# Selective scan: one third of the u*B inputs made by ScalarE and TensorE, 18 of 32 products with C on GpSimd

## The reference, cut to what matters

```python
def step(h, inp):
    dt_t, B_t, C_t, x_t = inp
    dA = jnp.exp(dt_t[..., None] * A)
    h = dA * h + (dt_t * x_t)[..., None] * B_t[:, None, :]
    y = jnp.einsum('bds,bs->bd', h, C_t)
    return (h, y)
```

## Time and profile before

| | us |
|---|---|
| median of 3 runs | 933.68 (931.17 to 933.75) |
| the profiled execution | 933.33 |
| its span | 931.5 |
| mean granted PE clock | 0.92 of full |

### The profile page before, as it was taken

One profiled execution on the slowest core, in us unless ns is written; L12 is line 12 of the kernel. 1 busy time (PEld: TensorE's weight loads), 2 busy tenths in 40 slices (PEclk: granted clock), 3 DMA queues, 4 the chain that ended last, 5 costly groups with the idle time before them and its releaser, 6 DMA issues. The chain is left out here.

```text
span 931.5 us, 13443 instructions
## 1 busy us (share of the span) xinstructions
PE 769.6 (83%) x3784; PEld 504.4 (54%) x3784; DVE 764.1 (82%) x1265; ACT 543.2 (58%) x1309; POOL 652.2 (70%) x447
## 2 busy tenths in 40 slices
PE   4889887899999994787878788786988767777998
PEld 2566653566666662435554465454645554422786
DVE  3588867668889995848989899998999989999743
ACT  1588854544444441676778776676875776552332
POOL 3178850467777782239989989999998999995000
PEclk9899998799999997997978699889998978899999
DMA  3000007499879836316557545655456555552001
GB/s 116 1 1 1 0 16 316 162 421 357 298 272 362 310 132 200 73 48 166 154 153 198 169 130 158 185 143 162 143 161 174 158 154 156 169 156 67 1 1 46
DMA packets 66307, 141.76 MB, mean 152 GB/s; under 512 B 11649, under 2 KB 22273, under 8 KB 64065
## 3 DMA queue, kind: packets, MB, share of 16 engines
q1 hardware_dynamic: 56432, 117.62, 41.6%
q0 software_dynamic: 6048, 18.59, 5.6%
q10 hardware_dynamic: 3760, 4.78, 1.5%
HBM read 129.92 MB, written 11.04 MB: 151 GB/s over the span
## 5 line engine op out<-in xcount | busy, mean ns | idle before, releaser
L2078 POOL TENSOR_TENSOR uB<-u,rows_B 128x1024 f32<-128x1024 f32 x127 | 298.4, 2359 | 0.0
L2296 DVE TENSOR_TENSOR_SCAN da<-da,uB 128x512 f32<-128x512 f32 x160 | 193.2, 1220 | 20.6 <-ACT da L2180 19.3
L2321 PE MATMUL ya<-ident,hV 128*128 128x128 f32 x560 | 100.0, 311 | 45.7 <-DVE hV L2195 45.5
L2088 POOL TENSOR_TENSOR hP<-hS,rows_C 128x512 f32<-128x512 f32 x96 | 122.2, 1273 | 18.2 <-DVE hS L2293 12.2
L2321 PEld LDWEIGHTS ya<-ident,hV 128*128 128x128 f32 x560 | 74.7, 159 | 97.7 <-DVE hV L2195 68.8
L2293 DVE TENSOR_TENSOR_SCAN hS<-da,uB 128x512 f32<-128x512 f32 x96 | 115.8, 1206 | 7.1 <-issue 3.7
L2195 DVE TENSOR_TENSOR hV<-da,rows_C 128x512 f32<-128x512 f32 x160 | 107.0, 669 | 0.6 <-DMA rows_C<-bc_rows 0.6
L1139 POOL DMA_INDIRECT xg<-x_rows,li x63 | 73.2, 1161 | 46.6 <-DVE li L1001 22.6
L1230 PE MATMUL gups<-wring,xT 128*128 128x448 f32 x252 | 105.0, 539 | 0.3 <-issue 0.3
L2179 ACT ACTIVATE da<-zero 128x2 f32<-128x2 f32 x160 | 27.7, 173 | 126.4 <-DVE hV L2195 125.7
L2180 ACT ACTIVATE da<-dt,fm_A 128x510 f32<-128x510 f32 x128 | 85.1, 674 | 0.0
(11 more groups left out here) (419 smaller groups left out, 1692.5 us busy)
## 6 DMA issues: line engine op xcount, KB each, us to landing
rows_B<-bc_rows SPq DMA_DIRECT2D x128, 256.0 KB, 3.7
rows_C<-bc_rows SPq DMA_DIRECT2D x128, 256.0 KB, 4.3
wring<-in_moe_own SPq DMA_DIRECT2D x31, 704.0 KB, 6.2
wring<-in_moe_two SPq DMA_DIRECT2D x16, 1024.0 KB, 15.1
rows_sum<-y_rows SPq DMA_DIRECT2D x6, 512.0 KB, 8.4
lut_i<-in_lut_idx SPq DMA_DIRECT2D x1, 2160.0 KB, 8.6
x_rows<-xnw ACTq DMA_DIRECT2D x1, 1280.0 KB, 5.2
x<-in_x SPq DMA_DIRECT2D x4, 256.0 KB, 3.7
```

What stands on the lines that cost most here:

```text
L2078: e.tensor_tensor(uB[:, r % UPAIRS, :, :], u[:, d:d + 2, :], RB[:, r % BROWS, :].unsqueeze(1).broadcast_to([P, 2, HALF]), ALU.mult).then_i ...
L2088: e.tensor_tensor(hP[:, k % PBUF, :], hS[:, k % HBUF, :], RC[:, row % CROWS, :], ALU.mult).then_inc(s_hp, 1)
L2296: e.tensor_tensor_scan(a[:, way], a[:, way], uB[:, r % UPAIRS, b, way], 0.0, ALU.mult, ALU.add).then_inc(s_sc, 1)
L2321: mm = e.matmul(ya[n % 2][:, part], at[:, part], g.ident[:, :], start=False, stop=False, is_transpose=True, skip_group_check=True)
```

## The change

Only the scan changes.

1. In segments 1 to 3, for states 4, 7, 10, 13 and 14 of each pair (`TURNED`), POOL no longer makes u*B and SP no longer loads the row of B. PE turns u of both blocks (columns become partitions), ACT keeps that as `uT` and the turned B as `bT`. Then ACT makes the turned u*B, four copies of 128x256 with a scale per partition, into `uBT` (2 buffers). PE turns it back, four transposes per step, into the bank `da` that is three steps old (`input_back`).
2. For these steps the decay goes to SBUF (`das`, 3 buffers), and the scan takes decay from SBUF and input from PSUM.
3. In segments 1 to 3 POOL takes 18 of the 32 products with C of a pair instead of 12. PE adds them BACK = 5 steps later instead of 4. CBUF falls from 4 to 3, HBUF rises from 4 to 5, PBUF and LATE stay.
4. The space comes from `lutw`: the table is stored to HBM by SP ahead of the first row and loaded again by ACT's queue at step 2 of the last segment, where the weights' inputs `hh` and `hl` lay.
5. silu(z) of a segment moves from step 1 of its own to step 29 of it, directly ahead of silu(x) of the next, which moves from 33 to 29.

```diff
-UPAIRS, CBUF, PBUF, DABUF, HBUF = 3, 4, 3, 3, 4
-LATE = 4
+UPAIRS, CBUF, PBUF, DABUF, HBUF = 3, 3, 3, 3, 5
+FIRST_TURNED, TURNED, UTBUF, DSBUF = 1, (4, 7, 10, 13, 14), 2, 3
+LATE, BACK = 4, 5
 def on_pool(n):
-    return n % PSTEP % 7 in (1, 3, 5) and n % PSTEP < PSTEP - LATE
+    m = n % PSTEP
+    if m >= PSTEP - LATE:
+        return False
+    return m % 7 in (1, 3, 5) if n // SSTEP < FIRST_TURNED else m % 3 != 2 and m > 0
+def turned_row(r):
+    return 2 * r // SSTEP >= FIRST_TURNED and r % DS in TURNED
 def summed(pair):
+    first, end = pair * PSTEP, (pair + 1) * PSTEP
     order = []
-    for n in range(pair * PSTEP, (pair + 1) * PSTEP):
-        if not on_pool(n):
-            order.append(n)
-        if n - LATE >= pair * PSTEP and on_pool(n - LATE):
-            order.append(n - LATE)
+    for n in range(first, end + BACK):
+        if n < end and not on_pool(n):
+            order.append((n, n))
+        if n - BACK >= first and on_pool(n - BACK):
+            order.append((n, n - BACK))
     return order
...
+        def turns_tensor(e, seg):
+            if seg >= FIRST_TURNED:
+                yield 0
+                turn_u(e, 2 * seg, 0)
+                yield 29
+                turn_u(e, 2 * seg + 1, 0)
+                yield 31
+                turn_u(e, 2 * seg + 1, 1)
+            if FIRST_TURNED <= seg + 1 < NSEG:
+                yield 62
+                turn_rows(e, seg + 1)
+                yield 63
+                turn_u(e, 2 * seg + 2, 1)
+        def turns_scalar(e, seg):
+            if seg >= FIRST_TURNED:
+                yield 0
+                keep_u(e, 2 * seg, 1)
+                yield 2
+                keep_u(e, 2 * seg, 0)
+                yield from turned_scalar(e, 2 * seg)
+                yield 31
+                keep_u(e, 2 * seg + 1, 0)
+                yield 33
+                keep_u(e, 2 * seg + 1, 1)
+                yield from turned_scalar(e, 2 * seg + 1)
+            if FIRST_TURNED <= seg + 1 < NSEG:
+                yield 63
+                keep_rows(e, seg + 1)
...
+        def turned_input(e, row, q):
+            t, seg = TROWS.index(row), 2 * row // SSTEP
+            if q == 0:
+                e.wait_ge(s_ut, 2 * TURN_PAIRS.index(row // DS) + 2)
+                e.wait_ge(s_bt, seg - FIRST_TURNED + 1)
+                if t >= UTBUF:
+                    e.wait_ge(s_tr, 2 * (t - UTBUF) + 2)
+            s = row % DS
+            i = e.activation(sc.uBT[:, t % UTBUF, q, :], sc.uT[:, q, :, :].rearrange("p b d -> p (b d)"), ACT.Identity,
+                             scale=sc.bT[:, q, s:s + 1])
+            if q == HALF // P - 1:
+                i.then_inc(s_ub2, 1)
+        def turned_scalar(e, pair):
+            base = pair % 2 * PSTEP
+            for s in TURNED:
+                for q in range(HALF // P):
+                    yield base + 2 * s - 5 + q
+                    turned_input(e, pair * DS + s, q)
+        def input_back(e, n):
+            t = TSTEPS.index(n)
+            e.wait_ge(s_ub2, t // 2 + 1)
+            bank_free(e, n - DABUF)
+            for q in range(HALF // P):
+                mm = e.transpose(da[n % DABUF][:, q * P:(q + 1) * P], sc.uBT[:, t // 2 % UTBUF, q, n % 2 * P:(n % 2 + 1) * P],
+                                 g.ident[:, :])
+            mm.then_inc(s_tr, 1)
...
@@ project_scalar
+            if k > FIRST_TURNED:
+                yield 29
+                silu_z(e, k - 1)
+                silu_input(e, k)
             yield 31
             keep_dt(e, k - 1, 3)
-            yield 33
-            silu_input(e, k)
+            if k <= FIRST_TURNED:
+                yield 33
+                silu_input(e, k)
...
@@ the adds on PE
-                    begun = 0
-                    for i, n in enumerate(summed(pair)):
+                    begun, next_turned = 0, [n for n in TSTEPS if n // PSTEP == pair]
+                    for i, (at, n) in enumerate(summed(pair)):
+                        while next_turned and next_turned[0] - DABUF <= at:
+                            input_back(e, next_turned.pop(0))
```

More of the change, by code:

```diff
@@ L1306, in on_pool, with turned_rows, plain_rows @@
 def on_pool(n):
-    return n % PSTEP % 7 in (1, 3, 5) and n % PSTEP < PSTEP - LATE
+    m = n % PSTEP
+    if m >= PSTEP - LATE:
+        return False
+    return m % 7 in (1, 3, 5) if n // SSTEP < FIRST_TURNED else m % 3 != 2 and m > 0
 def pool_steps(n):
-    full, part = divmod(n, PSTEP)
-    return full * sum(on_pool(i) for i in range(PSTEP)) + sum(on_pool(i) for i in range(part))
+    return sum(on_pool(i) for i in range(n))
 def vector_steps(n):
     return n - pool_steps(n)
+def turned_row(r):
+    return 2 * r // SSTEP >= FIRST_TURNED and r % DS in TURNED
+def turned_rows(r):
+    return sum(turned_row(i) for i in range(r))
+def plain_rows(r):
+    return r - turned_rows(r)
 def place(n):
@@ L1404, in mamba @@
         XB = [S0, S1]
+        UTB = [[S1, S0], [S1, S1]]
+        TURN_PAIRS = range(2 * FIRST_TURNED, 2 * NSEG)
         INB = [[S0, S1], [S2, da[0]]]
@@ L1408, in mamba @@
         HB = NB // NH
-        mv, sm = c.sb(ctx, "ln3_mv", [P, NB, 2]), c.sb(ctx, "ln3_sm", [P, 4, NB])
+        mv, sm = c.over("ln3_mv", [P, NB, 2], sc.rest), c.over("ln3_sm", [P, 4, NB], sc.rest, skip=8 * NB)
         half_of = lambda seg: slice(seg % 2 * HALF, (seg % 2 + 1) * HALF)
@@ L1726, in diagonals, with bank_free, turn_u @@
                              scale=ws[1].cvw[:, m, t:t + 1]).then_inc(s_dg, 1)
+        def bank_free(e, past):
+            if on_pool(past):
+                e.wait_ge(s_sc, past + 1)
+            else:
+                e.wait_ge(s_hv, vector_steps(past + 1))
+        def turn_u(e, pair, b):
+            seg, d = pair // 2, 2 * (pair % 2) + b
+            at, to = TURN_PAIRS.index(pair), UTB[pair % 2][b]
+            e.wait_ge(s_u, DB * seg + d + 1)
+            if pair % 2 == 0:
+                e.wait_ge(s_dtc, DB * seg + d + 1)
+                if b == 0:
+                    e.wait_ge(s_bt, seg - FIRST_TURNED + 1)
+            elif b == 0 and seg + 1 < NSEG:
+                e.wait_ge(s_cv, DB * (seg + 1))
+            elif b:
+                e.wait_ge(s_ut, 2 * at + 1)
+            for q in range(HALF // P):
+                part = slice(q * P, (q + 1) * P)
+                mm = e.matmul(to[:, part], u[:, d, part], g.ident[:, :], start=q == 0, stop=True, is_transpose=True,
+                              skip_group_check=True)
+            mm.then_inc(s_tu, 1)
@@ L2757, in build, with in_table @@
             sc.yT = c.sb(mm, "y_turned", [P, 2, HALF])
+            spare_at = c.at[g.lutw.name]
+            def in_table(name, shape):
+                nonlocal spare_at
+                made = nc.alloc_sbuf_tensor_at(name, shape, F32, offset=spare_at)
+                spare_at += 4 * int(np.prod(shape[1:]))
+                assert spare_at <= c.at[g.lutw.name] + c.size[g.lutw.name]
+                return made
+            sc.uT = in_table("u_turned", [P, HALF // P, 2, P])
+            sc.uBT = in_table("uB_turned", [P, UTBUF, HALF // P, 2 * P])
+            sc.das = [in_table(f"decay{i}", [P, HALF]) for i in range(DSBUF - 1)]
             at = 0
```

117 lines of the change are left out of this document (89 added, 28 removed).

## The result

The changed kernel takes **1065.94 us** (1062.46 to 1068.03, 4 runs) against 933.71 for the kernel before (4 runs): the ratio is 1.1434, 95% interval 1.1403 to 1.1465. The forecast was slower, 980 us with a range of 938 to 1008. The direction was right and so was the wait that it named; the size was off by 86 us, and where that came from is worked out behind the experiments.

The account below looks back on a forecast made before the run. POOL and DVE were taken to bound the kernel. A pair walked to 58.9 us, plus 2 for side tasks and 1 for turned u, made 61.9; six pairs added 46.8 to 933.3, giving 980.1 us, range 938 to 1008.

Parts of the forecast that it names:

- What bounds the kernel now: Scan stretch, 417 to 852 us: POOL (416.0 of 435 us) and DVE (406.5) are both within 7% of full.
- the walk: One pair of channel blocks in segments 1 to 3, summed step by step: 58.9 us against 54.1 before.
- What is taken away and added: Six changed pairs: POOL falls by 25.3 us, DVE by 21.2; ACT's scaled copies add 56, PE's 60 transpose sets 26 to 40.
- The wait that the change turns on: With three buffers, POOL's products with C wait for PE's adds behind later DVE products: at least 12.1 us per six steps.
- The failed term is PE's part of the loop: Between DVE's product and POOL's: transposes back, two adds and signals, within 3.59 us from scan 12 to POOL's start.
- the loop: Scan 12 to 18 and 18 to 24: DVE product, PE's adds, POOL's products, next scan; at least 12.1 us each.
- The rest of the pair: Scan 24 to next 12: 11.3 us to 30, 3.6 to next pair, 6.7 to 4, 13.1 to 12.
- A: The loop isn't there in the six pairs; POOL's sum rules, 25.2 us less, 908 us; chance 0.13.
- B: The loop holds only scan 12 to 24, other 20 steps at POOL's price: 933 to 960 us; chance 0.16.
- C: In-order queues of PE and ACT bind beyond the loop: 65 to 66 us a pair, 1000 to 1010 us; chance 0.11.
- The sign that it named: In the scan stretch, PE over 95% busy or DVE waiting mainly for ACT or PE would show C.
- Signs: Right if POOL idles tens of us for PE, gates stand about 60 us apart, POOL's share falls to some 80%.

Follow-up runs that it names:

- four buffers: Changed kernel with four instead of three buffers for POOL's products with C and one hS buffer fewer (PBUF 4, HBUF 4): 968.05 us, ratio 1.038.
- PE awake, order mended: Changed kernel plus zero matmuls ahead of transposes back, both steps turned back at once, side tasks behind both adds; three buffers, BACK 5: 1051.18 us, ratio 1.112.
- best kernel: Changed kernel with PBUF 4, HBUF 5, DSBUF 2, BACK 4, both steps back at once, side tasks behind both adds, turned u kept later: 955.03 us, ratio 1.0103.
- kernel with PE awake: Changed kernel with three matmuls of zeros on PE ahead of each turned row's transposes back: 1060.23 us, ratio 1.1256.

## Why the prediction was off, step by step

By stretches of a pair, mean of six, worked out from the start of every scan (the last pair up to the end of its last scan):

| us | scan 0 to 4 | 4 to 12 | 12 to 18 | 18 to 24 | 24 to 30 | 30 to next 0 | pair |
|---|---|---|---|---|---|---|---|
| before | 9.9 | 11.6 | 9.6 | 9.6 | 10.0 | 3.4 | 54.1 |
| walked in the prediction | 6.7 | 13.1 | 12.1 | 12.1 | 11.3 | 3.6 | 58.9 |
| after | 8.8 | 14.9 | 15.0 | 15.1 | 15.8 | 5.4 | 75.0 |
| four buffers | 8.1 | 11.7 | 10.4 | 10.4 | 13.1 | 5.6 | 59.2 |
| BACK 4 | 8.2 | 13.2 | 10.4 | 10.6 | 12.4 | 4.5 | 59.3 |
| PE awake, order mended | 8.4 | 14.9 | 13.0 | 13.3 | 15.7 | 5.7 | 71.0 |
| best kernel (BACK 4, four buffers) | 8.3 | 11.0 | 10.1 | 9.8 | 12.3 | 3.7 | 55.1 |

**What bounds the kernel now.** Right: POOL and DVE at the top, POOL's waits for PE small.

**Where the miss lies.** A pair was forecast at 61.9 us (58.9 walked, 3 on top) and took 75.0. Against the walk 16.1 us are missing: 5.9 in the two loops from scan 12 to 24, 4.5 from 24 to 30, and 5.7 at the change of pair and in steps 4 to 12.

**What is taken away and added.** Right for POOL, the scans and ACT. The work on POOL fell by 23.7 us in the stretch (25.3 forecast), and the scans kept their length with their operands exchanged. ACT's copies took 58.4 us (56). PE was priced too low: its 60 sets back were busy 45.5 us where 26 to 40 were forecast, and all of its work in the stretch 397.7 where the most was 387. The silus were booked at 0 and are worth 6 us.

**The wait that the change turns on.** Right, and shown from two sides. A fourth buffer takes 94.9 us out of S and BACK 4 takes 93.9, each with the lower clock's share in it, and without turned rows the loop stays (S = 422.4).

**The failed term is PE's part of the loop.** It was walked as 1.79 us between the end of the DVE product and POOL's start, plus 0.4 for side tasks on average, and it measured 4.82 (646.82 to 651.64). Over all twelve loops the part from the scan to POOL is 2.3 us longer than walked. The prices came from rows in which PE had the upper clock, as its transposes 0.43 us apart in the earlier trace rows do, and the walk priced the last pair's adds, 1.02 us as plain matmuls in the kernel before, as transposes too; and though the page shows granted clocks of 0.7 to 0.9 by slice, the sum did not ask which clock PE would have just there. The loop itself makes PE idle ahead of it. Of the 3.0 us that a loop is longer than walked, the clock holds 1.3 to 1.9 (kernel with PE awake) and the side tasks 0.8 to 1.1; with the second transposes moved as well the loop falls to 12.5 in segments 1 and 2. The Trainium skill (TensorE: Matmul & The Clock Gate, Part 1) says that an idle TensorE drops to half its clock and gets it back by sustained work; the trace agrees (0.50 right behind 3.81 us of idle time), and the page was not weighed in the prediction.

**The rest of the pair.** Scan 24 to the next 12 was walked to 34.7 us and measured 44.9. With four buffers it is 38.4, so about 6 us of the gap go with the loop, and in the best kernel 35.3. One link that the walk left out can be read in pair 3. It took the DVE product of step 26 to end 5.8 us after scan 24, and it ended 10.84 after: DVE may issue it only behind scan 27, and scan 27 waited for its transposes back, which stood on PE behind the add of 23, side tasks and the add of 18:

```profile
663.80 1.91 PE L1579 MATMUL side<-u,ident 128*128 128x512 f32 x2
664.73 1.42 PE L1453 MATMUL side<-hh,wh_in 128*128 128x512 f32 x1
...
668.46 0.60 PE L1869 MATMUL da<-ident,uB_turned 128*128 128x128 f32 x4
...
669.15 1.22 DVE L2469 TENSOR_TENSOR_SCAN hS<-decay_last,da 128x512 f32<-128x512 f32 x1 [2.71 <-PE da L1869]
```

In the six pairs that product ended 9.0 to 10.9 us after scan 24. The prediction allowed one side task of at most 1.02 us between two adds; here they take 2.7 us (663.80 to 666.47). At the change of pair ACT waited 6.58 us for PE's turning of B (681.77), and the next pair's first scan 2.75 us for ACT (682.76). Neither PE's three edits nor ScalarE's placing shortened this part with three buffers. In the kernel with PE awake the trace shows a chain through the side tasks there, DVE's input product waiting for PE (2.07 us at 666.65) and ACT waiting 5.87 us for PE's z rows at 669.22 before its next decay; and the added matmuls of zeros (2.74 us at 669.46) stand ahead of transposes for which DVE then waits 3.09 us (672.74), so that run can't tell what the order alone would give. How the 10 us divide among these links was not shown and stays open.

**The rivals** of the prediction (its B and C are not those of the experiments). A (908 us) fell with 142.7 us of POOL's waits. B (gaps below 57 us) fell. C put in-order queues beyond the loop and ended at 1010 us. The sign that it named is there: of 162 us that DVE waited, 59.0 are for ACT and 49.1 for PE, more than for u*B. So forecast and C were both partly right, and C too used PE at the upper clock. (Its sum has a slip: 58.9 with 4, 2 and 1 to 2 makes 65.9 to 66.9 a pair, 1004 to 1010 us.) The range failed because each of its bounds came from the same undisturbed prices: the upper end should have had PE at the lower clock: 0.40 to 0.46 us more for each of three sets of four transposes (0.88 from start to start instead of 0.43; 1.06 for the last instead of 0.60 to 0.66) and 0.9 for a side task (1.92 instead of 1.02), over 2 us a loop.

**Signs.** POOL's idle time put down to PE came as forecast in kind. POOL's share of the stretch fell to 69% and not some 80%, and the gates stand 71 to 78 us apart and not about 60.

**Segment 0 and the tail** were booked at 0 within 1 us and took 2.9 and 3.8. Segment 0 took 110.8 us in "Both steps of a row turned back at once", which doesn't differ from the changed kernel there, so most of the 2.9 may be spread between executions. In the tail DVE waits 2.96 us for the last add (987.37), where the gate of before came at once.
